# Last attention of a four-layer network: the scores go to SBUF, already scaled, on their way through VectorE's maximum

## The chip, the cores and the metric

The program runs on one core of one Trainium2 chip. The metric is the device time of one execution in microseconds (us), lower is better.

## The reference

The network has four layers, each an attention and a feed-forward part, on x of 16 x 128 x 256 (16 tiles of 128 rows, width 256). The change is mostly in the attention of the last layer. There all 2048 rows attend to all 2048 context rows, with 16 heads of width 16, and queries, keys, values and probabilities are rounded to integer steps:

```python
q = (x @ Wq + bq).reshape(1, B * N, H, hd)
kv = (cond @ Wkv + bkv).reshape(1, -1, 2, H, hd)
...
q = _fq_sym(q, axis=-1)
k = _fq_sym(k, axis=-1)
v = _fq_sym(v, axis=2)
attn = jnp.einsum('bhqd,bhkd->bhqk', q, k)
attn = jax.nn.softmax(attn.astype(jnp.float32), axis=-1)
attn = _fq_unsigned(attn, axis=-1)
out = jnp.einsum('bhqk,bhkd->bhqd', attn, v)
```

The other stages that the change touches are the two mixtures of experts (layers 0 and 3) and the ternary feed-forward part with its masked attention (layer 1).

## The kernel before, in words

The program is a row of stages, each a block in which the engines run their own instruction lists and meet by semaphores: attention 0, a grouped attention, the first mixture of experts (`moe`, called with `ternary`, so `first` is true), the ternary part (`mask_bit`), attention 2, a low-rank part, `qkv3` (queries, keys and values of the last attention), `attend3` (the last attention), and `moe` again (`first` false). No planner is at work; every order is written out by hand in the loops.

`attend3` works in units. A unit u is one half of the 2048 keys (1024 of them) for one head and one tile of 128 rows; two units make a pair (a head), 32 units a tile, 512 units the stage. For each unit:

- `score` (TensorE, L2743) multiplies the turned keys and queries into two of six PSUM banks; `S[:, u % 3]` is a ring of three units.
- `maximum` (VectorE, L2673 for an even unit in one instruction, L2677 for an odd one, bank by bank) takes the row's maximum, and `bias` (L2682, L2684), once a pair, makes of the three maxima the bias of the exponential: minus the maximum times the step, plus ln 255.
- `exp` (ScalarE, L2653) reads the scores from PSUM, scales them by the row's step `steps[:, 0]`, adds the bias and writes integers of 0 to 255 into `ex` (a ring of four), with the sum of the row beside it (its own short instruction, ACTIVATION_READ_ACCUMULATOR). It waits for the bias of its pair.
- `turn` (TensorE, L2755) turns the eight 128 x 128 blocks of `ex` into one PSUM bank, `TPW`. There is one such bank, so `turn(u)` waits for `evacuated` of unit u - 1.
- `evacuate` copies `TPW` to `pw` in SBUF: even units on ScalarE (L2658), odd ones on VectorE (L2688).
- `attend` (TensorE, L2765) multiplies by the values into the bank `O`.

TensorE's list is, for u = 0, 1, ...: `score(u)`, `turn(u - 4)`, `attend(u - 5)`. `score(u)` waits until exp of unit u - 3 has left its PSUM banks. VectorE's list is, for each pair: maximum, maximum, bias, copy of the odd unit before; at a tile's start the row steps and the scaling of the tile before (L2693 to L2710) come in between. ScalarE's list is exp(u), copy of u - 2, exp(u + 1). GpSimd has nothing to do in the stage but to clear old semaphores.

`keep_busy` (L162) issues n matmuls of a 128 x 128 identity by 512 columns into a bank that nobody reads. It stands before in `qkv3` and in `mask_bit` (L3226: 12 in the first round, L3228: 7 in each of the others, between `down` of the round and `turn_b`, L3146, which waits for ScalarE's quantised rows).

Of the kernel before, what the change touches and what calls it, by code (L numbers as in the profile page):

```python
# [10 lines left out]
ALU = mybir.AluOpType  # L11
# [5 lines left out]
P = 128  # L17
# [1039 lines left out]
def moe(nc, k, layout, x_in, src_in, out, arena, load_next, hand, ternary=None):  # L1057
# [11 lines left out]
    with ExitStack() as ctx:  # L1069
# [383 lines left out]
        def _(pe):  # L1453
# [72 lines left out]

            for i in range(NI + 2):
# [3 lines left out]
                for j in range(PAIR):  # L1531
                    if mid:
                        gate_up(i - 1, j * NC)
                    if front and not first and j == 0:
                        project(i)
                    if front and not first and j == 1:
                        logits(i)
# [4 lines left out]
                    if first and front and j == 0:  # L1542
                        turn_tok(i)
                    if mid:
                        gate_up(i - 1, j * NC + (1 if first or j else 2))
# [1037 lines left out]
def attend3(nc, k, qT_in, steps, out, KT, V, v_step, load_next, hand, qt):  # L2583


    W3 = 3 * 32
# [6 lines left out]
    with ExitStack() as ctx:  # L2593
        def sb(name, shape, dt=F32):
# [4 lines left out]
            even_scores odd_scores unit_max row_max bias exped turned evacuated  # L2599
# [5 lines left out]
        mx = sb("mx", [P, 2, NH, 6])  # L2605
# [35 lines left out]
        @block.gpsimd  # L2641
        def _(pool):
            clear_spent(nc, k)

        @block.scalar
        def _(act):
            def exp(u):
                t, h = u // UN, u % UN // 2
                if u % 2 == 0:
                    act.wait_ge(s["bias"], u // 2 + 1)  # L2650
                if u >= 4:
                    act.wait_ge(s["turned"], u - 3)
                nc.scalar.activation(ex[:, u % 4], S[:, u % 3], ACT.Exp, bias=mx[:, t % 2, h, 4:5], scale=steps[:, 0, t, h:h + 1],  # L2653
                                     accum_out=sums[:, t % 2, u % 2, h:h + 1]).then_inc(s["exped"], 1)
# [5 lines left out]
            for u in range(0, NU, 2):  # L2660
                exp(u)
                if u >= 2:
                    evacuate(u - 2)
                exp(u + 1)
            evacuate(NU - 2)

        @block.vector
        def _(dve):
            def maximum(u):
                t, h = u // UN, u % UN // 2  # L2670
                if u % 2 == 0:
                    dve.wait_ge(s["even_scores"], u // 2 + 1)
                    nc.vector.tensor_reduce(mx[:, t % 2, h, 0:1], S[:, u % 3], X, ALU.max).then_inc(s["unit_max"], 1)  # L2673
                else:
                    for b in range(2):
                        dve.wait_ge(s["odd_scores"], u - u % 2 + b + 1)
                        nc.vector.tensor_reduce(mx[:, t % 2, h, 1 + b:2 + b], S[:, u % 3, b * 512:(b + 1) * 512], X, ALU.max).then_inc(s["unit_max"], 1)  # L2677

            def bias(u):
                t, h = u // UN, u % UN // 2  # L2680
                dve.wait_ge(s["unit_max"], u // 2 * 3 + 3)
                nc.vector.tensor_reduce(mx[:, t % 2, h, 3:4], mx[:, t % 2, h, 0:3], X, ALU.max).then_inc(s["row_max"], 1)  # L2682
                dve.wait_ge(s["row_max"], u // 2 + 1)
                nc.vector.tensor_scalar(mx[:, t % 2, h, 4:5], mx[:, t % 2, h, 3:4], steps[:, 1, t, h:h + 1], LN255, ALU.mult, ALU.add).then_inc(s["bias"], 1)  # L2684
# [27 lines left out]
            for u in range(0, NU, 2):  # L2712
# [5 lines left out]
                bias(u + 1)  # L2718
                if u >= 4:
                    evacuate(u - 3)  # L2720
# [4 lines left out]
            evacuate(NU - 3)  # L2725
# [6 lines left out]
        def _(pe):  # L2732
            def score(u):
# [5 lines left out]
                if u >= 3:  # L2739
                    pe.wait_ge(s["exped"], u - 2)  # L2740
                for b in range(2):
# [3 lines left out]
                    if u % 2:  # L2745
                        last.then_inc(s["odd_scores"], 1)
                if u % 2 == 0:
                    last.then_inc(s["even_scores"], 1)
# [29 lines left out]
def mask_bit(nc, k, x_in, x_out, ctx_T, ctx_rows, masks, arena, load_next, hand, ternary):  # L2778
# [7 lines left out]
    with ExitStack() as ctx:  # L2786
# [336 lines left out]
        def _(pe):  # L3123
# [90 lines left out]
            for i in range(NI + 2):  # L3214
# [12 lines left out]
                elif i < NI:  # L3227
                    keep_busy(nc, k, 6, 7)  # L3228
# [173 lines left out]
```

## Time and profile before

| | |
|---|---|
| median of 3 runs | 2972.43 us (2972.11 to 2978.95) |
| the profiled execution, own time | 2973.31 us |
| its span, first to last instruction | 2971.5 us |
| PE, DVE, ACT, POOL busy | 84%, 69%, 57%, 18% of the span |
| mean granted TensorE clock | 0.945 of full |
| `attend3` | from 1673 to 2611 us of the span |

PE is TensorE (PEld its weight loads), DVE is VectorE, ACT is ScalarE, POOL is GpSimd. A row of a timeline has the start, the duration, engine, line, operation, output <- input, how many were merged, and in brackets how long the engine had stood idle and what ended that. A row of a group has the count, the busy time and the mean of one.

### The profile page before, as it was taken

The page shows a single profiled execution, that of the slowest core. Times are in us where ns is not written, and L with a number is a line of the kernel's source. Part 1 is how long each engine was busy: PE and PEld are TensorE (multiplying, and loading weights), DVE is VectorE, ACT ScalarE, POOL GpSimd, SP SyncE. Part 2 cuts the span into 40 slices and gives each one's busy share as a digit, 9 for nine tenths or more (in the row PEclk, how much of TensorE's full clock was granted, in tenths as well). Part 3 has the DMA queues.
Part 4 walks back from the last instruction along what each step waited for, and adds up shares of the span by engine and source line. Part 5 has one row for each costly group of instructions (what it writes and reads, how often), then busy time and mean ns, then how long its engine had stood idle before and what let it go on. Part 6 is the DMA issues. An engine that isn't in the chain of part 4 may idle for free. (4 is left out here: it accounts for less than half of the span.)

```text
span 2971.5 us, 51879 instructions
## 1 busy us (share of the span) xinstructions
PE 2484.5 (84%) x19857; PEld 1665.4 (56%) x19865; DVE 2036.8 (69%) x4916; ACT 1698.3 (57%) x3295; POOL 530.8 (18%) x401
## 2 busy tenths in 40 slices
PE   6978999988999776897977677777777777789999
PEld 5646676765666444675655444444444444456666
DVE  6847667653343686665757899999999999943231
ACT  4635767653333464443434688888888888822232
POOL 2124343321221233222311300000000000011121
PEclk9989999998999777999999899999999999989999
DMA  3120000002000212101013300000000000000000
GB/s 138 39 77 8 11 8 19 6 4 79 22 22 11 93 36 72 30 28 41 29 54 103 111 9 14 10 9 9 16 16 9 14 10 9 3 27 22 11 11 11
DMA packets 58949, 92.89 MB, mean 31 GB/s; under 512 B 5440, under 2 KB 54608, under 8 KB 57680
## 3 DMA queue, kind: packets, MB, share of 16 engines
q1 hardware_dynamic: 58704, 89.57, 9.0%
q8 instruction: 161, 2.64, 0.4%
q14 instruction: 84, 0.69, 0.1%
HBM read 66.48 MB, written 23.07 MB: 30 GB/s over the span
## 5 line engine op out<-in xcount | busy, mean ns | idle before, releaser
L2653 ACT ACTIVATE attend_ex<-psum,attend_mx,queries_step 128x1024 uint16<-128x1024 f32 x512 | 618.4, 1208 | 122.8 <-DVE attend_mx L2684 122.8
L2755 PEld LDWEIGHTS psum<-ident_b,attend_ex 128*128 128x128 bf16 x4096 | 253.2, 100 | 399.6 <-issue 398.3
L2755 PE MATMUL psum<-ident_b,attend_ex 128*128 128x128 bf16 x4096 | 329.8, 226 | 150.4 <-DVE attend_pw L2688 120.3
L2743 PE MATMUL psum<-keys_turned,queries_ahead 96*128 96x512 bf16 x1024 | 328.4, 405 | 76.5 <-ACT attend_ex L2653 72.9
L1502 PE MATMUL psum<-arena,moe_tokT 128*128 128x512 f32 (+2 forms) x896 | 361.7, 549 | 2.7 <-DVE moe_h L1389 2.7
L2677 DVE TENSOR_REDUCE attend_mx<-psum 128x1 f32<-128x512 f32 x512 | 329.5, 685 | 26.6 <-PE psum L2743 8.7
L2673 DVE TENSOR_REDUCE attend_mx<-psum 128x1 f32<-128x1024 f32 x256 | 310.9, 1215 | 4.9 <-PE psum L2743 4.6
L1389 DVE TENSOR_TENSOR moe_h<-moe_sg,psum 128x512 f32<-128x512 f32 (+1 forms) x112 | 69.9, 625 | 265.7 <-PE psum L1502 258.6
L1502 PEld LDWEIGHTS psum<-arena,moe_tokT 128*128 128x128 f32 x896 | 166.6, 192 | 139.1 <-issue 121.3
L1236 ACT ACTIVATE moe_sg<-psum 128x512 f32<-128x512 f32 (+1 forms) x112 | 61.4, 548 | 291.6 <-PE psum L1502 287.3
L2765 PE MATMUL psum<-values,attend_pw 128*128 128x16 f16 x4096 | 180.9, 171 | 1.4 <-DVE attend_pw L2688 0.6
L1524 PE MATMUL psum<-arena,moe_hT 128*128 128x256 f32 (+1 forms) x800 | 178.9, 380 | 2.7 <-ACT moe_hT L1248 1.6
L1170 POOL IOTA moe_index<- 128x8 f32 x2 | 0.3, 142 | 998.4 <-POOLq L2593 946.1
L2688 DVE COPY attend_pw<-psum 128x512 f32<-128x512 f32 x256 | 174.2, 680 | 5.0 <-PE psum L2755 5.0
L1524 PEld LDWEIGHTS psum<-arena,moe_hT 128*128 128x128 f32 (+1 forms) x800 | 150.8, 190 | 28.2 <-issue 3.3
L2765 PEld LDWEIGHTS psum<-values,attend_pw 128*128 128x128 f16 x4096 | 161.2, 98 | 3.7 <-issue 3.0
L2658 ACT COPY attend_pw<-psum 128x512 f32<-128x512 f32 x256 | 150.0, 586 | 21.9 <-PE psum L2755 8.5
L1194 POOL TENSOR_TENSOR moe_h<-moe_h,moe_cw 128x1408 f32<-128x1408 f32 (+1 forms) x32 | 90.6, 2832 | 375.3 <-DVE moe_h L1389 368.5
L1246 ACT COPY moe_hT<-psum 128x512 f32<-128x512 f32 (+1 forms) x112 | 54.1, 527 | 108.7 <-PE psum L1514 108.7
L2743 PEld LDWEIGHTS psum<-keys_turned,queries_ahead 96*128 96x128 bf16 x1024 | 59.4, 98 | 99.3 <-ACT attend_ex L2653 90.2
L793 POOL TENSOR_TENSOR gqa_nq<-gqa_nq,neg_half 128x20 f32<-128x20 f32 x16 | 88.2, 5514 | 148.1 <-DVE gqa_nq L911 148.1
L989 PE MATMUL psum<-arena,gqa_hT 128*128 128x512 f32 x256 | 113.2, 595 | 0.0
(453 smaller groups left out, 4848.3 us busy)
## 6 DMA issues: line engine op xcount, KB each, us to landing
residual<-stored_rows SPq DMA_DIRECT2D x48, 128.0 KB, 1.7
queries_turned<-queries_rows SPq DMA_DIRECT2D x16, 384.0 KB, 3.1
queries_ahead<-queries_turned SPq DMA_DIRECT2D x16, 384.0 KB, 3.3
arena<-in_moe SPq DMA_DIRECT2D x1, 5704.0 KB, 18.3
arena<-in_gqa SPq DMA_DIRECT2D x1, 5440.0 KB, 17.7
arena<-in_moe SPq DMA_DIRECT2D x1, 4360.0 KB, 13.3
xatt_ct<-in_ctx_T SPq DMA_DIRECT2D x32, 128.0 KB, 2.3
residual<-stored_rows SPq DMA_DIRECT2D x16, 256.0 KB, 2.1
```

The costliest lines, as they stand in the source:

```text
L989: last = nc.tensor.matmul(BIG[:, b], hT[:, ic], wq[:, ic, b * 512:(b + 1) * 512], start=ic == 0, stop=ic == DC - 1)
L1194: nc.gpsimd.tensor_tensor(hv, hv, cw[:, i % 2, j].unsqueeze(2).to_broadcast([P, SETS, I]), ALU.mult).then_inc(s["h_done"], 1)
L1502: last = nc.tensor.matmul(bank[:, q % 2, 0:size], tokT[:, i % 2, j, ic], wt[:, ic, at:at + size], start=ic == 0, stop=ic == DC - 1)
L1524: last = nc.tensor.matmul(YB[:, j * D:(j + 1) * D], hT[0:size, j, c], wd[0:size, c], start=c == 0, stop=c == DN - 1)
L2653: nc.scalar.activation(ex[:, u % 4], S[:, u % 3], ACT.Exp, bias=mx[:, t % 2, h, 4:5], scale=steps[:, 0, t, h:h + 1], accum_out=sums[:, t % ...
L2658: nc.scalar.copy(pw[:, u % 4], TPW).then_inc(s["evacuated"], 1)
L2673: nc.vector.tensor_reduce(mx[:, t % 2, h, 0:1], S[:, u % 3], X, ALU.max).then_inc(s["unit_max"], 1)
L2677: nc.vector.tensor_reduce(mx[:, t % 2, h, 1 + b:2 + b], S[:, u % 3, b * 512:(b + 1) * 512], X, ALU.max).then_inc(s["unit_max"], 1)
L2688: nc.vector.tensor_copy(pw[:, u % 4], TPW).then_inc(s["evacuated"], 1)
L2743: last = nc.tensor.matmul(S[:, u % 3, b * 512:(b + 1) * 512], qt[:, t % 2, h * P:(h + 1) * P], KT[:, c:c + 4, h // 2], start=True, stop=True)
L2755: last = nc.tensor.transpose(TP[:, c], counts[u % 4][:, c * P:(c + 1) * P], k["ident_b"][:])
L2765: last = nc.tensor.matmul(O[:, h * HD:(h + 1) * HD], pT[u % 4][:, c], V[:, kc, h * HD:(h + 1) * HD], start=kc == 0, stop=kc == B - 1)
```

## The change

In `attend3`, VectorE's maximum becomes one instruction a unit that also writes: `tensor_tensor_reduce` adds a broadcast zero to the scores, multiplies by the row's step, writes the 1024 results to `kept` in SBUF (a new ring of four units), and gives their maximum; the odd unit's takes the even one's maximum as its start value, so it waits for that. The row maximum and the bias on VectorE go (L2682, L2684); GpSimd makes the bias once a pair. `exp` reads `kept` and needs no scale. `score(u)` now waits for `kept` of unit u - 3, not for its exp. A new wait of the maximum keeps it four units ahead of exp at most. ScalarE copies three of four turned banks (units 0, 1, 2 modulo 4), VectorE every fourth.

Beside it, `keep_busy` matmuls are added: in `moe` before the loop (9 if `first`, else 3), after the first `turn_tok` if `first` (2), after the first `project` if not (14); in `mask_bit` 14 in place of 7.

```diff
+            keep_busy(nc, k, 0, 9 if first else 3)
             for i in range(NI + 2):
...
                     if front and not first and j == 0:
                         project(i)
+                        if i == 0:
+                            keep_busy(nc, k, 0, 14)
...
                     if first and front and j == 0:
                         turn_tok(i)
+                        if i == 0:
+                            keep_busy(nc, k, 0, 2)
...
+        zero = sb("zero", [P, 1])
+        kept = sb("kept", [P, 4, UK])
...
-            clear_spent(nc, k)
+            nc.gpsimd.memset(zero[:], 0.0).then_inc(s["zeroed"], 1)
+
+            def bias(n):
+                t, h = n // NH, n % NH
+                pool.wait_ge(s["kept"], 2 * n + 2)
+                nc.gpsimd.tensor_scalar(mx[:, t % 2, h, 2:3], mx[:, t % 2, h, 1:2], -1.0, LN255, ALU.mult, ALU.add).then_inc(s["bias"], 1)
+
+            for n in range(NU // 2):
+                bias(n)
+                if n == 4:
+                    clear_spent(nc, k)
...
-                nc.scalar.activation(ex[:, u % 4], S[:, u % 3], ACT.Exp, bias=mx[:, t % 2, h, 4:5], scale=steps[:, 0, t, h:h + 1],
+                nc.scalar.activation(ex[:, u % 4], kept[:, u % 4], ACT.Exp, bias=mx[:, t % 2, h, 2:3],
                                      accum_out=sums[:, t % 2, u % 2, h:h + 1]).then_inc(s["exped"], 1)
...
             for u in range(0, NU, 2):
                 exp(u)
-                if u >= 2:
-                    evacuate(u - 2)
+                if u % 4 == 2:
+                    evacuate(u - 1)
                 exp(u + 1)
-            evacuate(NU - 2)
+                evacuate(u)
...
+                t, h, half = u // UN, u % UN // 2, u % 2
+                best = mx[:, t % 2, h]
+                dve.wait_ge(s["scores"], u + 1)
+                if half:
+                    dve.wait_ge(s["kept"], u)
+                if u >= 4:
+                    dve.wait_ge(s["exped"], u - 3)
+                nc.vector.tensor_tensor_reduce(kept[:, u % 4], S[:, u % 3], zero[:].to_broadcast([P, UK]), steps[:, 0, t, h:h + 1], best[:, 0:1] if half else -3.0e38,
+                                               ALU.add, ALU.max, best[:, half:half + 1]).then_inc(s["kept"], 1)
...
                 maximum(u + 1)
-                bias(u + 1)
-                if u >= 4:
+                if u % 4 == 2 and u >= 4:
                     evacuate(u - 3)
...
                 if u >= 3:
-                    pe.wait_ge(s["exped"], u - 2)
+                    pe.wait_ge(s["kept"], u - 2)
...
                 elif i < NI:
-                    keep_busy(nc, k, 6, 7)
+                    keep_busy(nc, k, 6, 14)
```

## Rows read from the trace of the kernel before

**Rows 1.** The page, part 2: granted TensorE clock in 40 equal slices, tenths of full.

```profile
PEclk9989999998999777999999899999999999989999
```

**Rows 2.** Windows: busy us (count) of PE, PEld, DVE, ACT, POOL; clock; DMA.

```profile
959.00:1160.00 201.00, 145.23 (x690) 91.28 (x697) 136.01 (x400) 104.85 (x196) 54.26 (x41) 0.75 0.15 52
1673.00:2611.00 938.00, 710.46 (x9216) 436.18 (x9216) 885.53 (x1616) 789.67 (x1281) 0.00 (x0) 0.95 0.05 17
2611.00:2632.00 21.00, 13.20 (x34) 8.52 (x35) 7.25 (x42) 3.85 (x6) 3.42 (x5) 0.59 0.27 81
696.00:711.00 15.00, 9.26 (x25) 5.12 (x24) 7.43 (x43) 2.68 (x4) 4.16 (x7) 0.66 0.83 315
```

**Rows 3.** Timelines by engine, one pair of `attend3` near 2103 us.

```profile
2102.79 0.61 PE L2755 MATMUL psum<-ident_b,attend_ex 128*128 128x128 bf16 x8 [0.45 <-DVE attend_pw L2688]
2103.44 0.60 PE L2743 MATMUL psum<-keys_turned,queries_ahead 96*128 96x512 bf16 x2
2104.16 0.61 PE L2755 MATMUL psum<-ident_b,attend_ex 128*128 128x128 bf16 x8
...
2101.96 0.68 DVE L2688 COPY attend_pw<-psum 128x512 f32<-128x512 f32 x1
2102.56 1.21 DVE L2673 TENSOR_REDUCE attend_mx<-psum 128x1 f32<-128x1024 f32 x1
2103.86 1.29 DVE L2677 TENSOR_REDUCE attend_mx<-psum 128x1 f32<-128x512 f32 x2
2105.18 0.16 DVE L2682 TENSOR_REDUCE attend_mx<-attend_mx 128x1 f32<-128x3 f32 x1
2105.38 0.21 DVE L2684 TENSOR_SCALAR attend_mx<-attend_mx,queries_step 128x1 f32<-128x1 f32 x1
2105.51 0.68 DVE L2688 COPY attend_pw<-psum 128x512 f32<-128x512 f32 x1
...
2103.43 0.59 ACT L2658 COPY attend_pw<-psum 128x512 f32<-128x512 f32 x1
2103.92 1.21 ACT L2653 ACTIVATE attend_ex<-psum,attend_mx,queries_step 128x1024 uint16<-128x1024 f32 x1
2105.62 1.20 ACT L2653 ACTIVATE attend_ex<-psum,attend_mx,queries_step 128x1024 uint16<-128x1024 f32 x1 [0.41 <-DVE attend_mx L2684]
```

**Rows 4.** Timeline of PE at a tile's start.

```profile
1742.80 0.61 PE L2755 MATMUL psum<-ident_b,attend_ex 128*128 128x128 bf16 x8 [1.18 <-DVE attend_pw L2688]
...
1744.17 1.01 PE L2755 MATMUL psum<-ident_b,attend_ex 128*128 128x128 bf16 x8
```

**Rows 5.** DVE: tensor_tensor_reduce in the grouped attention (timeline), and the slowest 1024-element group.

```profile
236.34 0.29 DVE L933 CUSTOM_DVE_ANT_0 gqa_pr<-psum,gqa_cmask 128x128 f32<-128x128 f32 x1
...
236.56 0.28 DVE L933 CUSTOM_DVE_ANT_0 gqa_pr<-psum,gqa_cmask 128x128 f32<-128x128 f32 x1
...
L2490 DVE TENSOR_REDUCE qkv_vx<-qkv_vs 128x256 f32<-128x1024 f32 x4 | 7.5, 1886 | 0.0
```

**Rows 6.** Groups by line and form, ACT: a 1024-element ACTIVATE from SBUF with a bias column.

```profile
L2960 ACT ACTIVATE mbit_hq<-mbit_ag,minus_magic 128x1024 bf16<-128x1024 f32 x16 | 18.2, 1141 | 5.2 <-DVE mbit_ag L3092 5.2
```

**Rows 7.** Waits, 1024 to 1145 us in `mask_bit` (total us, times, longest), then two timeline rows.

```profile
PE psum L3146 <- ACT mbit_bq L2954: 10.9, 6, 2.0
...
DVE mbit_x L3018 <- PE psum L3210: 7.2, 5, 1.5
DVE mbit_xs L3003 <- PE psum L3172: 4.5, 5, 0.9
...
1067.36 0.69 POOL L2888 TENSOR_TENSOR mbit_xs<-mbit_xs,neg_half 128x2 f32<-128x2 f32 x1
1067.49 1.67 PE L166 MATMUL psum<-ident_b 128*128 128x512 bf16 x7
```

**Rows 8.** Timeline of PE at the head of either `moe`.

```profile
703.29 1.88 PE L1490 MATMUL psum<-arena,moe_tokT 128*128 128x8 f32 x8 [0.68 <-ACT moe_tokT L1225]
...
2622.46 1.11 PE L1483 MATMUL psum<-ident,moe_tok 128*128 128x128 f32 x4 [4.73 <-DVE moe_tok L1329]
```

More of the change, by code:

```diff
@@ L2598, in attend3 @@
             weights_next q_loaded0 q_loaded1 o_stored0 o_stored1
-            even_scores odd_scores unit_max row_max bias exped turned evacuated
+            zeroed scores kept bias exped turned evacuated
             attended both row_recip probs_step scaled o_done""")
@@ L2604, in attend3 @@
         O = k["psum"][:, 7, 0:D]
-        mx = sb("mx", [P, 2, NH, 6])
+        zero = sb("zero", [P, 1])
+        kept = sb("kept", [P, 4, UK])
+        mx = sb("mx", [P, 2, NH, 3])
         sums = sb("sums", [P, 2, 2, NH])
@@ L2661, in _ @@
                 exp(u)
-                if u >= 2:
-                    evacuate(u - 2)
+                if u % 4 == 2:
+                    evacuate(u - 1)
                 exp(u + 1)
-            evacuate(NU - 2)
+                evacuate(u)
         @block.vector
         def _(dve):
+            dve.wait_ge(s["zeroed"], 1)
             def maximum(u):
[L2670 to L2684, printed above, removed]
+                t, h, half = u // UN, u % UN // 2, u % 2
[7 more added lines that the diff above has]
+                                               ALU.add, ALU.max, best[:, half:half + 1]).then_inc(s["kept"], 1)
             def evacuate(u):
@@ L2724, in _ @@
                     scale_columns(t - 1)
-            evacuate(NU - 3)
             row_steps(B - 1)
@@ L2744, in score @@
                                             KT[:, c:c + 4, h // 2], start=True, stop=True)
[L2745 to L2748, printed above, removed]
+                last.then_inc(s["scores"], 1)
             def turn(u):
```

## The prediction, made blind

> **What bounds the kernel now.** I read the page's slices first, then the table of windows, then the timeline of the last attention engine by engine, then the waits and timelines of the stages that get more `keep_busy`.
>
> The clock row [rows 1] is at nine tenths or full nearly everywhere and dips to seven tenths in three slices, which are `mask_bit`; the windows [rows 2] give it 0.75 over 201 us there, 0.95 in `attend3`, and 0.59 and 0.66 at the heads of the two `moe`. `attend3` is 938 of the 2971.5 us. In it VectorE is busy 885.5 us (94%), ScalarE 789.7 (84%), TensorE 710.5 (76%). The stage is VectorE's.
>
> A pair [rows 3] shows how. VectorE starts the even maximum at 2102.56, the odd one at 2103.86, the two small bias instructions at 2105.18 and 2105.38, the copy at 2105.51, and the next pair would start one copy step later, at 2105.51 + (2102.56 - 2101.96) = 2106.11. The period is 3.55; the unrounded starts give 3.54, the distance of the copies 3.55. I use 3.54. 256 pairs make 906 us; the other 32 of the 938 are the ramp and, 16 times, the row steps and scaling of a finished tile with the slow clock that follows [rows 4]. ScalarE has room: its odd exp ends about 2105.22 and the next starts at 2105.62, having waited 0.41 us for the bias. TensorE's waits are of one kind: `turn` at 2102.79 starts 0.83 after the start of VectorE's copy (2101.96), and at 2104.16 it starts 0.73 after that of ScalarE's (2103.43). There is one bank for turned blocks, so turn, copy, turn, copy form a single file whoever makes the copy.
>
> **VectorE after the change.** Per pair it loses 1.30 + 1.32 (maxima), 0.20 + 0.13 (bias) and half of its copies. It gains two `tensor_tensor_reduce`. The nearest row is the same operation in the grouped attention, PSUM and an f32 tensor of SBUF in, SBUF out: 128 columns start to start in 0.22 [rows 5]. The maximum of 1024 takes 1.21 and one of 512 0.6 to 0.65 (two in 1.29) [rows 3], so a column costs about 1.04 ns and 896 more of them 0.93. That gives 1.15. The new one has a scale column, and an odd one also a start column; a small instruction with a scalar column takes 0.05 more than one without (0.21 against 0.16 [rows 3]), so I take 1.21 and 1.27. The odd one waits for the even one's result, which adds about 0.12 (no overlap with the one before): 1.33 + 1.27 + half a copy step 0.30 = 2.90 per pair instead of 3.54. The lower bound is 1.15 each without any cost of columns or wait (2.60 a pair). The upper bound is the slowest instruction on 1024 elements of this profile, 1.89 [rows 5]: 1.95 + 1.89 + 0.30 = 4.14. The row of the same operation is far nearer, and I take its value.
>
> The Trainium skill, "Vector Engine (DVE) Microarchitecture Reference", section "Points that are easy to get wrong", says that one shape of two-source DVE instruction with an accumulator runs at half throughput when both sources are non-bf16 tensors of SBUF. Here one source is PSUM, and the 0.22 us for 128 columns [rows 5] would not hold 128 columns at 2.1 ns (0.27 us); the rule would hold only if the broadcast zero counted otherwise. By it the pair would be about 5 us.
>
> **ScalarE.** exp reads SBUF and has one operand column instead of two. The nearest row, 1024 from SBUF with a bias column and 16-bit output, takes 1.141 [rows 6] against 1.21: 0.07 less. The unhindered step of an exp with its accumulator is now 1.19 (1.21, plus a short second instruction, less the overlaps); I take 1.13, and 1.19 as the upper end (reading SBUF saves nothing). A copy's step is 0.49 (2103.43 to 2103.92). Four units with three copies: 4 x 1.13 + 3 x 0.49 = 5.99, or 3.00 a pair. So ScalarE, not VectorE, has most work in its list, yet neither sets the pace alone.
>
> **TensorE and the single file.** Start to start, turn to the next score is 0.65 (2102.79 to 2103.44), of which turn to attend about 0.45. Score to a VectorE instruction that needs both banks: 0.60 + 0.04. Turn to a copy on ScalarE: 0.64. Score now goes as soon as `kept` of three units before is there, which it is. The chain that closes over four units: ScalarE's copy of unit 5 starts; turn 6 0.73 later; score 11 0.65; VectorE's odd instruction on unit 11 0.64; its copy of unit 7 1.27 (it stands behind that instruction in the list); turn 8 0.83; ScalarE's copy of 8 0.64; then exp 10 and the copy of 9, 0.49 + 1.13. Sum 6.38 for four units, 3.19 a pair: longer than ScalarE's own 5.99 and VectorE's 5.80. Everything else has slack. GpSimd's bias is hidden: exp of unit 6 starts 1.27 + 0.83 + 0.64 + 0.49 = 3.23 after the start of the odd maximum, whose result is there after 1.36; a small GpSimd instruction with a power takes 0.69 [rows 7], which leaves 1.1 us. Without that cover each 0.1 us would cost up to 26 us over the 256 pairs. The memset and the one `dve.wait` at the stage's head are under 1 us, and clearing semaphores after pair 4 runs under the same slack or costs about a microsecond once. SP's loads wait for the same exps as before.
>
> Gain: 256 x (3.54 - 3.19) = 90 us. Less at the tile starts: today TensorE stands 1.18 us there and soon after a turn takes 1.01 instead of 0.61 [rows 4], for some 8 to 10 us of each 58. The tile's small VectorE instructions remain, so I expect the same fall. At half clock TensorE needs about 1.9 a unit (score, turn, attend doubled from about 1.08, less fixed parts), 3.84 a pair, which is above 3.19 and was only a little above 3.54. Over 7 us of each tile that costs about 0.4 us more than today: 16 x 0.4 = 6. Net 84 us; the stage comes to about 854.
>
> **More keep_busy.** One at full clock takes 1.67 / 7 = 0.24 [rows 7].
> - `mask_bit`: 7 more take 1.6 to 1.7 us in each of seven rounds, 11.4 in all. TensorE stands 10.9 us over six such places, up to 2.0 each, waiting for ScalarE [rows 7], so the time is free while the clock is full. If the clock then stays up, VectorE's waits for TensorE, 7.2 + 4.5 us over five rounds (2.3 a round) [rows 7], shrink; at most 7 x 2.3 = 16. Uncovered at half clock they would cost up to 7 x 1.4 = 10. I take half the bound, -8, since TensorE still stands elsewhere in the round.
> - `moe` first: the head runs at 0.66 clock for 15 us [rows 2]; eight small products take 1.88 [rows 8] and could take half. Lost there: about 0.34 x 2 x 9.3 busy us / 2 = 3 us at most. The 9 lie under the wait for the first rows. I take -2.
> - `moe` second: 3 at half clock (0.48 each, twice 0.24) stand ahead of the first turn, +1.3 on the path. The 14 fill a wait of 4.73 us [rows 8]: 3.4 us at full clock, 6.7 at half. If the clock is up, 13.2 busy us at 0.59 [rows 2] lose up to 5 us less. Net -2.5, bounds -4 and +3.
>
> Sum: 84 + 8 + 2 + 2.5 = 96.5 less. Against the profiled execution, 2973.3 (span 2971.5 and 1.8 around it), that is 2876.8; the median shown is 0.9 below that execution, so 2876.
>
> **The rivals.**
> - *VectorE stays the bound*, its new instruction slower than the row says (write and reduction together, the columns dearer). It takes over from 3.19 at a mean step of (3.19 - 0.30) / 2 = 1.45. At 1.6 each the pair is 3.5, nothing is won in the stage, and the time is about 2960. For it: no row has this operation at 1024 columns. Against: [rows 5].
> - *Slower than before*: the same instruction above (3.54 - 0.30) / 2 = 1.62. At the bound 4.14 the stage grows by 256 x 0.60 = 154, and the time is about 3115. It is one mechanism, at one place. By the Trainium skill's rule on that shape, cited above, it would be more still.
> - *ScalarE alone is the bound*: the chain above is relaxed because the order shifts by itself and the clock stays up through the tile starts. 3.00 a pair: 256 x 0.54 = 138, less nothing at the tiles, and 12 elsewhere: about 2822 to 2835. For it: TensorE's idle per pair falls. Against: one turned bank, in fixed order.
> - *The clock falls oftener*: with shorter and more irregular stops in `attend3` it is down a third of the time: 0.33 x 938 x (3.84 - 3.19) / 3.54 = 57 us lost. About 2930. Against it: TensorE is busier than before per time.
> - *keep_busy does nothing or harm*: -12.5 becomes 0 to +13; 2889 to 2902. This lies in the range.
>
> **How the numbers follow.** Forecast 0.68; ScalarE alone 0.08; VectorE still the bound 0.09 (of it a third within 0.3%); clock oftener 0.09; slower 0.06. Predicted 2876. The likeliest case alone spans 3.10 to 3.28 a pair (-23, +23) and keep_busy (-8, +25): 2850 to 2915. For 8 in 10 I go to 2842 and 2922, part of the way into the cases on either side. 0.3% is 9 us, about what a measurement can tell here: faster is below 2963. Faster 0.90, same 0.04, slower 0.06.
>
> **What would show it right or wrong.** In the changed profile the new VectorE instruction should take 1.28 to 1.36 with starts 1.2 to 1.35 apart; exp 1.14; a period of four units of 6.4; `attend3` 854 us; ScalarE busy some 90% of it, VectorE about 92% with short waits for TensorE; exp never waiting long for GpSimd. Each turn should start 0.73 or 0.83 after a copy's start. `mask_bit`'s clock should be above 0.75 and its round under 20.4 us. The prediction is wrong if the new instruction's step is over 1.45, if exp waits for GpSimd's bias, or if the clock in `attend3` is well under 0.95.

## The result and the profile after

| | before | after |
|---|---|---|
| median (lowest to highest), us | 2974.70 (2972.11 to 2978.95), 4 runs | 2862.11 (2859.60 to 2864.67), 4 runs |
| ratio, 95% interval | | 0.962 (0.960 to 0.964) |
| span of the profiled execution | 2971.5 | 2857.8 |
| mean granted clock | 0.945 | 0.964 |
| `attend3` | 937.7 | 838.4 |

The kernel is 112.6 us faster. The forecast was 2876 (2842 to 2922) and 0.90 for faster, so the time is in the range and 14 us below the forecast. The line numbers of `attend3` have moved: score L2755, turn L2764, attend L2774, exp L2671, ScalarE's copy L2676, the new VectorE instruction L2697, its copy L2702, GpSimd's bias L2656.

The page of the kernel after, part 2, the granted clock in 40 slices (compare [rows 1]), and part 1, the busy times:

```profile
PE 2421.5 (85%) x19942; PEld 1626.7 (57%) x19942; DVE 1910.8 (67%) x4532; ACT 1689.4 (59%) x3423; POOL 581.8 (20%) x658
...
PEclk9989999999999889999999999999999999999999
```

The slices that stood at seven tenths are now at eight or more. The table of windows of the kernel after shows where. Its rows answer to [rows 2]: `attend3`, the head of the first `moe`, `mask_bit`, the head of the second `moe` (busy us and count of PE, PEld, DVE, ACT, POOL; clock; DMA):

```profile
1659.57:2498.00 838.43, 646.64 (x9216) 404.46 (x9216) 759.23 (x1232) 780.87 (x1409) 50.90 (x257) 0.98 0.06 19
696.00:711.00 15.00, 11.84 (x43) 5.54 (x43) 9.09 (x54) 3.87 (x6) 4.16 (x7) 1.00 0.86 322
955.00:1155.00 200.00, 144.62 (x754) 86.27 (x754) 138.51 (x412) 107.87 (x208) 56.34 (x45) 0.85 0.17 57
2498.00:2519.00 21.00, 17.30 (x53) 9.37 (x54) 7.27 (x43) 3.85 (x6) 3.42 (x5) 0.68 0.26 82
```

In `attend3` VectorE fell from 885.5 to 759.2 us, but the stage only to 838.4. VectorE is now busy 91% of it, ScalarE 93%, TensorE 77%: no engine fills it. The groups by line and form of the kernel after (count, busy us, mean ns of one, idle time before them and what ended it):

```profile
L2671 ACT ACTIVATE attend_ex<-attend_kept,attend_mx 128x1024 uint16<-128x1024 f32 x512 | 588.1, 1153 | 2.6 <-POOL attend_mx L2656 2.6
L2697 DVE CUSTOM_DVE_ANT_0 attend_kept<-psum,attend_zero,attend_mx 128x1024 f32<-128x1024 f32 x256 | 343.8, 1343 | 65.4 <-PE psum L2755 62.3
L2697 DVE CUSTOM_DVE_ANT_0 attend_kept<-psum,attend_zero,queries_step 128x1024 f32<-128x1024 f32 x256 | 327.5, 1279 | 11.9 <-PE psum L2755 9.3 <-issue 0.3
```

The even instruction takes 1.28 us, the odd one, which reads one more column, 1.34; exp takes 1.15 and waits for the bias 2.6 us in the whole program. What VectorE waits for is the next score. Timelines by engine of the kernel after, four units near 2103 us (compare [rows 3]):

```profile
2100.04 0.61 PE L2764 MATMUL psum<-ident_b,attend_ex 128*128 128x128 bf16 x8 [0.53 <-DVE attend_pw L2702]
...
2103.68 0.59 PE L2755 MATMUL psum<-keys_turned,queries_ahead 96*128 96x512 bf16 x2
...
2106.41 0.61 PE L2764 MATMUL psum<-ident_b,attend_ex 128*128 128x128 bf16 x8 [0.53 <-DVE attend_pw L2702]
...
2109.40 0.61 PE L2764 MATMUL psum<-ident_b,attend_ex 128*128 128x128 bf16 x8 [0.38 <-ACT attend_pw L2676]
...
2110.04 0.59 PE L2755 MATMUL psum<-keys_turned,queries_ahead 96*128 96x512 bf16 x2
...
2104.31 1.34 DVE L2697 CUSTOM_DVE_ANT_0 attend_kept<-psum,attend_zero,attend_mx 128x1024 f32<-128x1024 f32 x1 [0.32 <-PE psum L2755]
...
2105.57 0.69 DVE L2702 COPY attend_pw<-psum 128x512 f32<-128x512 f32 x1
2106.18 1.28 DVE L2697 CUSTOM_DVE_ANT_0 attend_kept<-psum,attend_zero,queries_step 128x1024 f32<-128x1024 f32 x1
...
2107.69 1.34 DVE L2697 CUSTOM_DVE_ANT_0 attend_kept<-psum,attend_zero,attend_mx 128x1024 f32<-128x1024 f32 x1 [0.23 <-PE psum L2755]
...
2110.67 1.34 DVE L2697 CUSTOM_DVE_ANT_0 attend_kept<-psum,attend_zero,attend_mx 128x1024 f32<-128x1024 f32 x1 [0.32 <-PE psum L2755]
...
2107.05 0.59 ACT L2676 COPY attend_pw<-psum 128x512 f32<-128x512 f32 x1 [0.28 <-PE psum L2764]
2107.53 1.15 ACT L2671 ACTIVATE attend_ex<-attend_kept,attend_mx 128x1024 uint16<-128x1024 f32 x1
...
2108.68 0.57 ACT L2676 COPY attend_pw<-psum 128x512 f32<-128x512 f32 x1
```

The turn behind VectorE's copy comes back after 2106.41 - 2100.04 = 6.37 us. The single file can be followed with a finger: score at 2103.68, VectorE's odd instruction 0.63 later (2104.31), its copy 1.26 later (2105.57), turn 0.84 later (2106.41), ScalarE's copy 0.64 later (2107.05), exp and the next copy 1.63 later (2108.68). From there the next turn (2109.40) and score (2110.04) follow 0.72 and 0.64 later, and VectorE's odd instruction (2110.67) 0.63 after that. The waits of the kernel after, 1690 to 2480 us (total us, times, longest), are the joints of that same file:

```profile
PE psum L2764 <- ACT attend_pw L2676: 82.2, 220, 0.4
PE psum L2764 <- DVE attend_pw L2702: 75.2, 120, 1.6
DVE attend_kept L2697 <- PE psum L2755: 63.4, 216, 1.0
ACT attend_pw L2676 <- PE psum L2764: 49.6, 127, 1.3
```

At a tile's start (compare [rows 4]) TensorE in the kernel after stands as long as before (1.20 us, once 1.55), yet the clock often stays up. Timeline of TensorE there:

```profile
1723.75 0.61 PE L2764 MATMUL psum<-ident_b,attend_ex 128*128 128x128 bf16 x8 [1.20 <-DVE attend_pw L2702]
...
1725.12 0.61 PE L2764 MATMUL psum<-ident_b,attend_ex 128*128 128x128 bf16 x8
```

The turn after the stop of 1.20 takes 0.61 and so does the next; before, that next one took 1.01. Before, matmuls at half clock follow all 15 tile starts inside the stage; after, 5 of 15. From one tile start to the next the kernel after takes 51.61 us without such a fall (twice 51.85 and 51.97) and 52.55 to 52.60 with one (before: 57.72 to 58.78, all with one). The count of 5 is that of one execution, the fastest of the four (2859.60 us, clock 0.964); the others, at 0.962 to 0.966, may have another.

Outside `attend3`, read off the starts of each stage's first instructions, `mask_bit` went from 190.2 to 182.3 us, the first `moe` from 275.95 to 273.1, and what follows `attend3` from 360.5 to 359.8. Stages that no edit touches, between `mask_bit` and `attend3`, are 2.4 us shorter in this execution; the profiled executions of kernels that are alike there differ by as much and more. Two timelines of TensorE in the kernel after, first in a round of `mask_bit` (compare [rows 7]), then at the head of the second `moe` (compare [rows 8]):

```profile
1042.34 3.19 PE L166 MATMUL psum<-ident_b 128*128 128x512 bf16 x14
...
1045.96 0.40 PE L3155 MATMUL psum<-ident_b,mbit_bq 128*128 128x128 bf16 x4 [0.44 <-ACT mbit_bq L2963]
...
2499.18 1.46 PE L166 MATMUL psum<-ident_b 128*128 128x512 bf16 x3 [2.14 <-POOL moe_index L1171]
...
2505.74 4.33 PE L166 MATMUL psum<-ident_b 128*128 128x512 bf16 x14
...
2510.68 0.66 PE L1483 MATMUL psum<-ident,moe_tok 128*128 128x128 f32 x4 [0.60 <-DVE moe_tok L1329]
```

In `mask_bit` 14 matmuls in 3.19 us (0.23 each, the level of 2.4 GHz) still end 0.44 before what they are to fill. In the second `moe` the first three take 0.49 each (the level of 1.2 GHz) and stand on the path; the 14 end 0.60 before the turned rows can start, and the four matmuls of L1483 then take 0.66 instead of 1.11. The clock was still down when the 14 began (0.31 each over the 4.33 us).

### The profile page after: what moved, and what is told of

Same layout as the page of the kernel before. It is cut to its first block and busy times, and to the rows that moved or that the text cites. A ratio compares the mean times of both kernels' runs of the same rounds, so it can differ in the third digit from the quotient of the medians.

```text
span 2857.8 us, 52551 instructions
## 1 busy us (share of the span) xinstructions
PE 2421.5 (85%) x19942; PEld 1626.7 (57%) x19942; DVE 1910.8 (67%) x4532; ACT 1689.4 (59%) x3423; POOL 581.8 (20%) x658
## 5 line engine op out<-in xcount | busy, mean ns | idle before, releaser
L2671 ACT ACTIVATE attend_ex<-attend_kept,attend_mx 128x1024 uint16<-128x1024 f32 x512 | 588.1, 1153 | 2.6 <-POOL attend_mx L2656 2.6
L2764 PEld LDWEIGHTS psum<-ident_b,attend_ex 128*128 128x128 bf16 x4096 | 241.7, 98 | 424.2 <-ACT attend_ex L2671 332.1
L2764 PE MATMUL psum<-ident_b,attend_ex 128*128 128x128 bf16 x4096 | 316.5, 221 | 186.2 <-ACT attend_pw L2676 87.9
L2697 DVE CUSTOM_DVE_ANT_0 attend_kept<-psum,attend_zero,attend_mx 128x1024 f32<-128x1024 f32 x256 | 343.8, 1343 | 65.4 <-PE psum L2755 62.3
L2697 DVE CUSTOM_DVE_ANT_0 attend_kept<-psum,attend_zero,queries_step 128x1024 f32<-128x1024 f32 x256 | 327.5, 1279 | 11.9 <-PE psum L2755 9.3
L2755 PE MATMUL psum<-keys_turned,queries_ahead 96*128 96x512 bf16 x1024 | 308.2, 383 | 3.1 <-PEq L2271 2.0
L2676 ACT COPY attend_pw<-psum 128x512 f32<-128x512 f32 x384 | 222.6, 580 | 51.7 <-PE psum L2764 51.5
L2656 POOL TENSOR_SCALAR attend_mx<-attend_mx 128x1 f32<-128x1 f32 x256 | 50.8, 199 | 779.0 <-DVE attend_mx L2697 779.0
L2774 PE MATMUL psum<-values,attend_pw 128*128 128x16 f16 x4096 | 178.9, 170 | 3.5 <-DVE stored_rows L2719 2.9
L2774 PEld LDWEIGHTS psum<-values,attend_pw 128*128 128x128 f16 x4096 | 157.4, 97 | 5.8 <-issue 5.1
L1039 PE MATMUL psum<-arena,gqa_oT 128*128 128x256 f32 x512 | 113.1, 379 | 0.0
L1039 PEld LDWEIGHTS psum<-arena,gqa_oT 128*128 128x128 f32 x512 | 97.3, 190 | 20.1 <-issue 7.7
```

What stands on the lines that cost most here:

```text
L1039: last = nc.tensor.matmul(Y, oT[:, c], wo[:, c], start=c == 0, stop=c == GH - 1)
L2671: nc.scalar.activation(ex[:, u % 4], kept[:, u % 4], ACT.Exp, bias=mx[:, t % 2, h, 2:3], accum_out=sums[:, t % 2, u % 2, h:h + 1]).then_in ...
L2676: nc.scalar.copy(pw[:, u % 4], TPW).then_inc(s["evacuated"], 1)
L2697: nc.vector.tensor_tensor_reduce(kept[:, u % 4], S[:, u % 3], zero[:].to_broadcast([P, UK]), steps[:, 0, t, h:h + 1], best[:, 0:1] if half ...
L2755: last = nc.tensor.matmul(S[:, u % 3, b * 512:(b + 1) * 512], qt[:, t % 2, h * P:(h + 1) * P], KT[:, c:c + 4, h // 2], start=True, stop=True)
L2764: last = nc.tensor.transpose(TP[:, c], counts[u % 4][:, c * P:(c + 1) * P], k["ident_b"][:])
```

## The experiments

Medians of four or five runs, except where one run is said. A median is beside the kernel before on the same chip, which was 2972.3 to 2974.4 in each. "Stage" is `attend3` in the profiled execution, and "falls" are the tile starts, of 15, that are followed by matmuls at half clock. Both are of one execution of each kernel, and that one isn't always near the median: it took 2878.66 us in (1), 2922.46 in (7) and 2874.99 in (10), the slowest of its kernel each time. The theory: the stage goes by the single file turn, copy, turn, copy through one bank, closed by VectorE's and ScalarE's lists, 6.38 us per four units. The rivals: the engine with most work, or the new instruction, or the clock.

**1 and 2. The two halves of the change.** The first run is the change without the added `keep_busy`; the second is the kernel before with only these.

```diff
-            keep_busy(nc, k, 0, 9 if first else 3)
...
-                        if i == 0:
-                            keep_busy(nc, k, 0, 14)
...
-                        if i == 0:
-                            keep_busy(nc, k, 0, 2)
...
-                    keep_busy(nc, k, 6, 14)
+                    keep_busy(nc, k, 6, 7)
```

> The changed kernel with all keep_busy as before (no matmuls added in either mixture, 7 a round in the ternary part). My reading of the two traces: the attention stage carries 99 of the 113 us and needs nothing of the rest, so the stage should again take about 838 us and the whole about 2875 us (2972 less 99), 0.5% above the changed kernel. Rival: part of the stage's 99 us comes from the clock that the added matmuls hold up elsewhere; then the stage would be above 845 us and the whole above 2880.

> The kernel before with only the added keep_busy. Prediction on record: 12.5 us less. By the landmarks of the two traces: 3 less in the first mixture, 8 less in the ternary part, under 1 less in the last mixture, and 2 less between the ternary part and the last attention, which no edit touches. I expect 12 to 14 us less than before, about 2960. Rival: the matmuls do nothing and the shift came with the attention: 2972.

Measured: attention alone 2873.94 (2871.79 to 2878.66), ratio 0.967 (0.966 to 0.969), 98.4 us less; stage 840.3, 7 falls; `mask_bit` 190.0. `keep_busy` alone 2960.73 (2957.91 to 2965.03), ratio 0.996 (0.995 to 0.998), 11.6 us less; stage 937.5; `mask_bit` 181.8, first `moe` 273.5. That is just under the 12 to 14 expected. The two add up to 110.0 of the 112.6. So seven eighths of the gain are the attention's, and the added matmuls are worth 12, as forecast (12.5).

**3. VectorE copies half of the banks, as before.** If the busiest engine set the pace, this would cost nothing: VectorE would be busy some 830 us of a stage of 838.

```diff
-                if u % 4 == 2:
-                    evacuate(u - 1)
+                if u >= 2:
+                    evacuate(u - 2)
                 exp(u + 1)
-                evacuate(u)
+            evacuate(NU - 2)
...
-                if u % 4 == 2 and u >= 4:
+                if u >= 4:
                     evacuate(u - 3)
...
+            evacuate(NU - 3)
```

> The changed kernel with the copies of the turned blocks split as before (ScalarE the even units, VectorE the odd ones). Theory, a chain through the single turned bank: every pair then has a copy that stands behind VectorE's odd instruction, and a pair takes 3.35 to 3.40 us against 3.19; the stage takes about 890 us and the whole about 2914. Rival, the busiest engine sets the pace: VectorE's list would be 1.33 + 1.27 + 0.60 = 3.20 a pair, ScalarE's falls to 2.8, and the stage stays within 5 us of 838.

Measured: 2919.49 (2917.16 to 2922.97), ratio 0.982 (0.981 to 0.984); stage 891.4 with VectorE busy 826.6 of it and ScalarE 732.9; 6 falls. Timelines of this kernel, VectorE and TensorE:

```profile
2151.81 0.69 DVE L2702 COPY attend_pw<-psum 128x512 f32<-128x512 f32 x1
...
2153.92 1.34 DVE L2697 CUSTOM_DVE_ANT_0 attend_kept<-psum,attend_zero,attend_mx 128x1024 f32<-128x1024 f32 x1 [0.22 <-PE psum L2756]
...
2155.19 0.69 DVE L2702 COPY attend_pw<-psum 128x512 f32<-128x512 f32 x1
...
2152.64 0.61 PE L2765 MATMUL psum<-ident_b,attend_ex 128*128 128x128 bf16 x8 [0.72 <-DVE attend_pw L2702]
...
2153.29 0.59 PE L2756 MATMUL psum<-keys_turned,queries_ahead 96*128 96x512 bf16 x2
```

The file is shorter in links but has VectorE's copy in each pair: copy 2151.81, turn 0.83 later, score 0.65 later, odd instruction 0.63 later, next copy 1.27 later: 3.38 us a pair with every engine idle at some point, against 3.19 after. The busiest-engine rival falls.

**4. Two banks for turned blocks.** Scores get a ring of two pairs of banks, the turned blocks two banks. Nothing is computed otherwise.

```diff
-        S = k["psum"][:, 0:6, :].rearrange("p (u b) c -> p u (b c)", b=2)
-        TPW = k["psum"][:, 6, :]
+        S = k["psum"][:, 0:4, :].rearrange("p (u b) c -> p u (b c)", b=2)
+        TPW = [k["psum"][:, 4 + r, :] for r in range(2)]
...
-                if u >= 3:
-                    pe.wait_ge(s["kept"], u - 2)
+                if u >= 2:
+                    pe.wait_ge(s["kept"], u - 1)
...
-                if u >= 1:
-                    pe.wait_ge(s["evacuated"], u)
+                if u >= 2:
+                    copied(u - 2)
```

Here `copied(u)` waits for the count of ScalarE's or VectorE's copies, whichever makes the copy of u.

> The changed kernel with two PSUM banks for turned blocks in turn, and the scores in a ring of two units instead of three (six banks in all as before with one to spare), the copies counted on two semaphores. Theory: the chain turn, copy, turn, copy is broken, and ScalarE's own list is left, 4 x 1.145 + 3 x 0.48 = 6.02 us for four units, 3.01 a pair instead of 3.19; the stage takes 785 to 795 us and the whole 2810 to 2820. Rival: the exps and maxima need the third unit of scores, or VectorE's waits for TensorE remain; then the pair stays at 3.15 or more and the whole at 2855 or more.

Measured: 2817.04 (2815.22 to 2820.41), ratio 0.948 (0.946 to 0.949), 155 us less than before and 45 less than the change; stage 790.0. The windows row of the stage, and the timeline of ScalarE, of this kernel:

```profile
1665.20:2455.20 790.00, 644.53 (x9216) 434.82 (x9216) 749.57 (x1232) 769.21 (x1409) 50.56 (x257) 0.98 0.06 20
```

```profile
2102.90 1.16 ACT L2671 ACTIVATE attend_ex<-attend_kept,attend_mx 128x1024 uint16<-128x1024 f32 x1
...
2104.04 1.14 ACT L2671 ACTIVATE attend_ex<-attend_kept,attend_mx 128x1024 uint16<-128x1024 f32 x1
...
2105.17 0.57 ACT L2676 COPY attend_pw<-psum 128x512 f32<-128x512 f32 x1
```

ScalarE is busy 97% of the stage, its steps back to back (1.14, 1.13), and a tile takes 48.87 us, 3.05 a pair: the 3.00 of ScalarE's own list and a little at the tile's start. With the single file gone, the stage is ScalarE's. This version beats both kernels. Whether a second bank would have helped the kernel before, no run shows.

**5. exp reads PSUM again.** The new VectorE instruction stays and still writes `kept`, which nobody reads. It asks what the store to SBUF is for.

```diff
-                nc.scalar.activation(ex[:, u % 4], kept[:, u % 4], ACT.Exp, bias=mx[:, t % 2, h, 2:3],
+                nc.scalar.activation(ex[:, u % 4], S[:, u % 3], ACT.Exp, bias=mx[:, t % 2, h, 2:3], scale=steps[:, 0, t, h:h + 1],
...
-                    pe.wait_ge(s["kept"], u - 2)
+                    pe.wait_ge(s["exped"], u - 2)
```

> The changed kernel, but exp reads the raw scores in PSUM with the scale column, as before the change, and score waits for exp of three units before; the scaled scores are written to SBUF and read by nobody. Everything else is as changed, so VectorE's list is as short. Theory: the gain hangs on the early release of PSUM; now exp, score, VectorE's instruction, GpSimd's bias and exp close a chain of about 5.4 us a pair, the stage takes about 1390 us and the whole about 3410. Rival: the gain is VectorE's shorter list alone; then the pair stays at about 3.2 to 3.3 (exp 0.06 longer), the whole at 2865 to 2885.

Measured, one run: 3772.35, against 2973.65 for the kernel before. Timeline of TensorE of this kernel:

```profile
2102.20 1.03 PE L2755 MATMUL psum<-keys_turned,queries_ahead 96*128 96x512 bf16 x2 [1.68 <-ACT attend_ex L2671]
```

and its windows row of the stage:

```profile
1670.80:3409.40 1738.60, 1064.03 (x9216) 706.69 (x9216) 768.32 (x1232) 837.86 (x1409) 50.50 (x257) 0.50 0.03 9
```

The score waits 1.68 us for an exp, as the theory of the banks' release said, and the sign is right. The size is not: 6.8 us a pair against the 5.4 expected. The chain is also another than expected; over two pairs it goes, twice, from exp (2194.99) to score 1.35 later, turn 0.83 later, ScalarE's copy 1.09 later and the next exp 0.49 later, and then from exp (2202.51) to score 1.36, VectorE's odd instruction 1.07, its copy 1.27, turn 0.83, ScalarE's copy 1.05 and exp 0.48 later: 13.58 in sum. GpSimd's bias is not on it, and TensorE's steps are long because it was granted half the clock (0.50) for nearly the whole 1739 us, which I had not foreseen. With the steps that the kernel after has at full clock (0.72, 0.64, 0.63) the same chain would take about 5.8 us a pair, by an estimate, so the clock makes up about 1.0 of the 1.4 that were missed. Why the clock stayed down no run here shows. exp from PSUM with two columns takes 1.21 and not 1.15, so the source and the column together are worth 0.06 (no run parts them).

**6 and 7. The same work at two places of VectorE's list.** An addition of 256 columns into a scratch tile (step 0.34) is put between the two halves of a pair, 256 times, or ahead of VectorE's copy, 127 times. The first place lies where VectorE waits for a score, the second on the file.

```diff
+                nc.vector.tensor_tensor(idle[:, u // 2 % 4], v_step[:], v_step[:], ALU.add)
                 maximum(u + 1)
```

```diff
                 if u % 4 == 2 and u >= 4:
+                    nc.vector.tensor_tensor(idle[:, u // 4 % 4], v_step[:], v_step[:], ALU.add)
                     evacuate(u - 3)
```

> The changed kernel with one more VectorE instruction a pair, an addition of 128 x 256 that nobody reads (a step of about 0.34 us), between the even and the odd unit's instruction: 256 of them, 87 us of work. Theory, the chain: VectorE waits 0.22 and 0.32 us for the scores at just that place, so most of it is hidden; the whole rises by 0 to 12 us, to 2862 to 2874. Rival, VectorE (91% busy) sets the pace: the whole rises by 60 to 87 us.

> The same instruction, but half as many (one in four units, 127 of them, 43 us of work), between the odd unit's instruction and the copy behind it. Theory: this place lies on the chain, so all of it shows: the whole rises by 40 to 44 us, to about 2905, more than twice the run with double the work. Rival, VectorE's sum sets the pace: it rises by about half of what the other run rises.

Measured: 2882.68 (2881.39 to 2883.21) and 2917.50 (2910.76 to 2922.46), ratios 0.969 (0.968 to 0.970) and 0.980 (0.978 to 0.982). That is 20.6 and 55.4 us above the change, where 0 to 12 and 40 to 44 were expected; stages 856.1 and 891.9, 15 falls in the first and 14 in the second. Timeline of VectorE, first of the kernel with 256 additions:

```profile
2060.85 0.69 DVE L2703 COPY attend_pw<-psum 128x512 f32<-128x512 f32 x1
...
2065.55 0.42 DVE L2732 TENSOR_TENSOR attend_idle<-values_step 128x256 f32<-128x256 f32 x1
2065.95 1.34 DVE L2698 CUSTOM_DVE_ANT_0 attend_kept<-psum,attend_zero,attend_mx 128x1024 f32<-128x1024 f32 x1
...
2067.22 0.69 DVE L2703 COPY attend_pw<-psum 128x512 f32<-128x512 f32 x1
```

and of the kernel with 127:

```profile
2100.94 0.68 DVE L2703 COPY attend_pw<-psum 128x512 f32<-128x512 f32 x1
...
2107.30 0.42 DVE L2734 TENSOR_TENSOR attend_idle<-values_step 128x256 f32<-128x256 f32 x1
2107.64 0.68 DVE L2703 COPY attend_pw<-psum 128x512 f32<-128x512 f32 x1
```

From copy to copy the first has 6.37 us, nothing more than the change although two additions were put in; the second has 6.70, its one addition in full (0.33). 127 times 0.33 are 42 us, so the chain's part is inside the 40 to 44 expected, and the whole is 11 above them. The rest of both lies at the tile starts. In the kernel with 256 additions the last six of the eight periods of a tile are, but for a few, 6.36 or 6.37; the first is 7.49, where the change has 7.04, and the second, behind a fall, 7.20 to 8.06, where the change has 6.37 without a fall and 7.30 to 7.36 with one. TensorE's stop there has grown from 1.20 to 1.65 (and to 1.53 or 1.54 with 127), and the clock falls each time but one: behind the stop of 1.53 that ends at 2178.82 in the kernel with 127, the turns take 0.61. I had expected 0 to 12 for the first and got 20.6: the inside of a tile was right, the tile starts were left out, in the second expectation too. Half the added work costs 2.7 times as much, so the sum of VectorE's work is not what counts.

**8. The stop at the tile's start filled, in the kernel before.** Four more score matmuls, repeating the two just made into the same banks, where TensorE stood 1.18 us [rows 4].

```diff
-                for b in range(2):
+                for b in (0, 1) * (3 if u > UN and u % UN == LAG + 2 else 1):
```

> The kernel before, with the scores of the seventh unit of each tile from the second computed three times (four matmuls more, 0.86 us), so that TensorE's stop of 1.18 us at the tile start is mostly filled. Theory: the clock falls there because of that stop; it then falls at few of the 15 tile starts, each tile takes about 57.2 instead of 58.0 us, and the whole is 10 to 15 us less than before, about 2960. Rival: the fall has another cause (the stops of 0.3 and 0.45 us in every pair); then the 15 falls stay and the time is within 3 us of before.

Measured: 2964.76 (2962.34 to 2965.88), ratio 0.997 (0.995 to 0.998), 9 us less, just under the 10 to 15 expected; stage 929.9; no fall at any of the 15 tile starts; tiles 57.52 to 57.54. Timeline of TensorE of this kernel:

```profile
1740.97 1.47 PE L2743 MATMUL psum<-keys_turned,queries_ahead 96*128 96x512 bf16 x6
1742.75 0.61 PE L2755 MATMUL psum<-ident_b,attend_ex 128*128 128x128 bf16 x8 [0.31 <-DVE attend_pw L2688]
...
1744.12 0.61 PE L2755 MATMUL psum<-ident_b,attend_ex 128*128 128x128 bf16 x8
```

The stop is 0.31 and the second turn takes 0.61 instead of 1.01. So the stop brings the fall on, and in the kernel before a fall was worth about half a microsecond (8 us over 15).

**9. Scores one unit earlier.** TensorE's list becomes `score(u)`, `turn(u - 5)`, `attend(u - 6)`.

```diff
-                if LAG <= u < NU + LAG:
-                    turn(u - LAG)
-                if u > LAG:
-                    attend(u - LAG - 1)
+                if AHEAD <= u < NU + AHEAD:
+                    turn(u - AHEAD)
+                if u > AHEAD:
+                    attend(u - AHEAD - 1)
```

with `AHEAD = LAG + 1`.

> The changed kernel with TensorE's list shifted: score(u), turn(u - 5), attend(u - 6) instead of 4 and 5; one turned bank and three units of scores as changed. No work is taken away and no buffer added. Theory: in the chain, score of unit 11 follows turn 6; now it is score 12 that does, unit 11's scores come a unit earlier, and VectorE's odd instruction no longer waits for them; the chain shortens to turn, copy, turn, copy with ScalarE's exps between, about 3.06 us a pair; the stage takes about 811 us and the whole about 2835. Rival: TensorE's order does not matter, since the single bank alone limits it; then the stage stays at 838 and the whole at 2862.

Measured: 2849.98 (2847.33 to 2853.96), ratio 0.959 (0.957 to 0.960); stage 827.2, 11 less than the change where 27 were expected; 7 falls. Timelines of this kernel, TensorE and VectorE:

```profile
2100.90 0.61 PE L2764 MATMUL psum<-ident_b,attend_ex 128*128 128x128 bf16 x8 [0.42 <-DVE attend_pw L2702]
...
2107.15 0.61 PE L2764 MATMUL psum<-ident_b,attend_ex 128*128 128x128 bf16 x8 [0.41 <-DVE attend_pw L2702]
...
2105.05 1.34 DVE L2697 CUSTOM_DVE_ANT_0 attend_kept<-psum,attend_zero,attend_mx 128x1024 f32<-128x1024 f32 x1 [0.35 <-ACT attend_ex L2671]
```

The period is 6.25. The order matters, as the theory says, but VectorE's odd instruction now waits 0.35 for an exp, that is, by the list, for a free place in `kept`: the ring of four became the next link. I had not counted it, and no run has a deeper ring.

**10. A later bias.** GpSimd does an addition of 256 columns (0.61 us) ahead of each bias; the prediction put the slack at 1.1.

```diff
                 pool.wait_ge(s["kept"], 2 * n + 2)
+                nc.gpsimd.tensor_tensor(idle[:, n % 4], v_step[:], v_step[:], ALU.add)
```

> The changed kernel with an addition of 128 x 256 on GpSimd (0.73 us, nobody reads it) ahead of each bias, so that the bias comes 0.7 us later, 256 times, 187 us of delay in sum. Prediction on record: exp of a pair starts some 1.1 us or more after its bias even if that took 0.69; the bias takes 0.19, so 0.7 more is hidden and the whole stays within 6 us of 2862. Rival: GpSimd's place between VectorE and ScalarE has no slack; then the whole rises by 50 us or more.

Measured: 2867.19 (2866.30 to 2874.99), ratio 0.964 (0.963 to 0.966), 5 us above the change; stage 843.6, 9 falls against 5. A tile without a fall takes 51.65 against 51.61, so inside a tile the later bias is hidden. The stage of the profiled execution is 5.2 us longer, of which the four more falls are most.

## Why the prediction was right, point by point

- **VectorE's instruction.** Steps of 1.21 and 1.27 were worked out from 128 columns and a cost per column; the trace has 2106.18 to 2107.38 (1.20) up to the start of the even one's short read, and 1.26 from odd instruction to copy. Durations 1.28 and 1.34 lie in the 1.28 to 1.36 given. It was extrapolated by a factor of eight in columns and held. The upper bound and the rival "slower" hung on 1.62. The Trainium skill, "Vector Engine (DVE) Microarchitecture Reference", section "Points that are easy to get wrong", has half throughput for one two-source shape, `S2S2D2_STT`, with two non-bf16 sources in SBUF; at PSUM and a broadcast column of SBUF the trace shows none of it, and no run has this instruction with both sources as full tensors in SBUF.
- **exp.** 1.15 against 1.14 forecast; its steps are 1.14 and 1.13. Right.
- **The chain.** 6.38 per four units forecast, 6.37 measured, and each link within 0.01: 0.72, 0.64, 0.63, 1.26, 0.84, 0.64, 1.63. Over 256 pairs that is 256 x 3.54 - 128 x 6.37 = 91 us, forecast 90. That it is a chain and not an engine was shown from four sides: moved copies cost 53 us (3), a second bank wins 48 in the stage and makes it ScalarE's (4), the same work costs nothing inside a tile at one place and its full length at another (6, 7), and a shift of one unit in TensorE's order wins 11 (9).
- **The bias.** Hidden, with at least 0.6 us to spare (10). The trace of the kernel after has GpSimd's bias at 2105.74 for 0.19 us and the exp that reads it at 2107.53, 1.6 us behind its end; 1.1 was forecast, with a bias of 0.69.
- **The tile starts: the term that was mis-sized.** The prediction had "I expect the same fall" at each and 0.4 us more for it than before, +6 us, for a stage of 854. Measured, everything in the stage outside the steady chain went from 937.7 - 906.2 = 31.5 us to 838.4 - 815.4 = 23.0, which is -8.5: the term is 14.5 off, and with it the total by 14. Two things make it up. A fall does cost more than before, 0.95 (52.55 against 51.61) instead of about 0.5, and that is the 0.4 more that the step gave; but only 5 tile starts of 15 had one, which saves 9.5. (The 0.4 itself was not worked out cleanly: 7 us at half clock, with 3.84 a pair against 3.54 and 3.19, give 0.6 more, which would have been 10 us and not 6. The clock was down for less than that: 5.7 us a tile on the mean before.) And a tile start without a fall costs 51.61 - 8 x 6.37 = 0.65, where the kernel before with the stop filled has 57.52 - 16 x 3.54 = 0.88, some 3.5 over 15. Ramps and roundings hold the remaining 1 to 2.
- **`keep_busy`.** Forecast -12.5, measured -11.6 by itself (2). On top of the attention's part (1) it is 2873.94 - 2862.11 = 11.8 by the two medians, or 112.6 - 98.4 = 14.2 by the two differences, since the kernel before took 2974.70 beside one and 2972.34 beside the other; two falls fewer in `attend3` are 2 of it. `mask_bit` -8 forecast, -7.9; first `moe` -2, -2.9; second `moe` -2.5, -0.7. In `mask_bit` the path was as described: the 14 still fit, rounds in which the clock stays full take 18.35 to 18.7 us and the others 19.9, where the kernel before has 20.4. That half of a bound of 16 came out within 0.1 is luck: no row said how many rounds would keep the clock. In the second `moe` the 3 at half clock cost their 1.3 or so (L1465 starts 1.25 behind the first of them), and the 14 gave little back. It doesn't take a low clock while they run: in the kernel with `keep_busy` alone (2) they ran at full clock, ended 1.70 before the turned rows, and the clock soon fell again: the eight products of L1490 took 1.58 there, 1.88 before. The clock of that head was 0.67, and what follows `attend3` took 360.8 us against 360.5. Timeline of TensorE of (2):

```profile
2602.97 3.19 PE L166 MATMUL psum<-ident_b 128*128 128x512 bf16 x14
2607.85 0.66 PE L1483 MATMUL psum<-ident,moe_tok 128*128 128x128 f32 x4 [1.70 <-DVE moe_tok L1329]
2609.19 1.58 PE L1490 MATMUL psum<-arena,moe_tokT 128*128 128x8 f32 x8 [0.68 <-ACT moe_tokT L1225]
```

In the kernel after, where they ended 0.60 before, L1490 took 1.06. What this small term took for granted is that the clock stays up behind a filled wait.
- **The rivals.** VectorE as bound: no, its steps are 1.20 and 1.26, not 1.45. ScalarE alone: not in the change, and yes once there are two banks, at 2817 where the rival said 2822 to 2835. "The clock falls oftener": the reverse in the change. It is a real danger all the same, as (5) shows, where the stage ran at half clock throughout.

What stays open: why a stop of 1.18 to 1.20 us brought the fall 15 times of 15 before, 5 of 15 after and 7 of 15 in (1) and (9). Filling it removes the fall (8), and longer stops of 1.53 and 1.65 bring it 14 and 15 times of 15 (7, 6), so the length counts. But before and after have the same length. The work around the stop differs between them, and no run here holds the length and varies that alone. It can't be the whole of it either: within the kernel after, ten starts with a stop of 1.20 kept the clock and four with the same stop and the same work around it did not (the fifth fall is at the stop of 1.55), so something that changes from tile to tile, such as the moment at which the stop comes, has a part.

## What to carry to other kernels

When an edit takes work from the busiest engine, don't divide the stage by the next engine's busy time: walk the closed chain through the buffer of which there is only one, link by link from start to start (here 6.38 for a measured 6.37, where ScalarE's busy time would have said 5.99). Then ask for a second such buffer: here a second bank for the turned blocks, with the ring of scores cut from three units to two, was worth another 45 us. Count what happens once per tile by itself, since an edit that leaves the steady part untouched can cost 20 us there.

## What the runs showed of the hardware

- `tensor_tensor_reduce` on 128 x 1024 with PSUM and a broadcast SBUF column in, f32 out to SBUF, takes 1.28 us with one column operand and 1.34 with two, with 0.08 for the accumulator's read. The plain maximum of the same 1024 took 1.21, so with the scaling and the store of every element to SBUF it is 0.07 to 0.13 dearer.
- TensorE's clock stayed at the lower level for nearly a whole stage (mean 0.50) while TensorE was busy 1064 of 1739 us, with three stops of 1.68 us in every two pairs of units (experiment 5). Before and after, busy 710 of 938 and 647 of 838 us with stops of about half a microsecond, it was at 0.95 and 0.98.
- A stop of 0.31 us in place of 1.18 at a tile's start kept the clock up 15 times of 15 (experiment 8).
